# A four-layer graph network on one core: second pass in a new order, step values loaded by turns, top-8 rounds in pieces of 832 columns

## The reference, cut to what matters

```python
e = leaky_relu(e, 0.2)                                   # 4 heads, by edge
mask = topk_mask(e, row, 8)                              # 8 largest of each node and head
e = where(mask, e, -inf)
ez = exp(e - segment_max(e, row)[row])
alpha = ez / segment_sum(ez, row)[row]
out = elu(segment_sum(alpha[:, :, None] * x_j, row))
x = layernorm(x + out)
```

## Time and profile before

| | us |
|---|---|
| median of 3 timed runs | 14784.25 (14783.6 to 14784.43) |
| the profiled execution | 14750.02 |
| its span | 14748.2 |
| second pass, first turn to last scatter | 3636 to 10346 |
| top-8 rounds | 12660 to 13263 |
| last gather | 14561 |

### The profile page before, as it was taken

How to read it: one execution, slowest core, us unless ns; L and a number is a source line. 1 busy time by engine, 2 the same in 40 slices (tenths; PEclk the granted TensorE clock), 3 DMA queues, 4 the chain that set the end, 5 groups by cost and what they waited for, 6 DMA issues and landing times. The chain is left out here.

```text
span 14748.2 us, 216662 instructions
## 1 busy us (share of the span) xinstructions
PE 7244.2 (49%) x43137; PEld 6163.1 (42%) x43138; DVE 7073.5 (48%) x13194; ACT 1344.8 (9%) x4579; POOL 6702.6 (45%) x7772
## 2 busy tenths in 40 slices
PE   6999995673222222222222222223599578207543
PEld 4787774562222222222222222223366367206433
DVE  6444445776222222222222222222488678997535
ACT  1111111111000000000000000000011100001000
POOL 3777771663222222222222222225588057897773
PEclk9999998996555555555555555555799689657655
DMA  4777773451111111111111111114998069318654
GB/s 131 204 207 205 205 204 87 137 153 58 60 59 62 59 62 61 60 62 59 61 59 61 59 62 59 60 59 153 163 257 257 10 179 259 102 38 225 189 157 124
DMA packets 2114489, 1742.91 MB, mean 118 GB/s; under 512 B 377267, under 2 KB 1838644, under 8 KB 2114212
## 3 DMA queue, kind: packets, MB, share of 16 engines
q1 hardware_dynamic: 1220182, 819.70, 19.1%
q10 hardware_dynamic: 708032, 472.39, 12.2%
q0 software_dynamic: 186160, 449.72, 11.1%
HBM read 1289.54 MB, written 453.29 MB: 118 GB/s over the span
## 5 line engine op out<-in xcount | busy, mean ns | idle before, releaser
L1125 POOL DMA_INDIRECT sorted<-m_rows,srci x1612 | 1569.9, 974 | 5166.8 <-SPq L1112 4731.6
L1181 PE MATMUL m_psx<-held,m_hot 128*128 x3608 | 939.7, 441 | 4740.7 <-DVE m_rows L1335 4740.7
L1181 PEld LDWEIGHTS m_psx<-held,m_hot 128*128 128x128 f32 x3608 | 807.9, 329 | 4816.2 <-issue 4816.1
L1324 DVE TENSOR_SCALAR m_hot<-m_keys,node 128x512 f32<-128x512 int32 x451 | 225.7, 500 | 4583.0 <-DMA m_keys<-dst_row 4569.8
L1577 POOL DMA_INDIRECT z_xg<-table,srci x1664 | 2082.5, 1252 | 507.2 <-issue 507.2
L443 POOL DMA_INDIRECT g_xg<-table,srci x1612 | 1607.0, 997 | 491.1 <-issue 461.6
L1637 PE MATMUL z_ps<-z_wrow,z_oh 128*128 128x132 f32 x3712 | 757.8, 372 | 619.1 <-DVE z_wrow L1790 313.9
L462 PE MATMUL g_psg<-g_wg,g_eT 128*128 128x136 f32 x3224 | 1027.5, 474 | 0.0
L1452 PE MATMUL n_ps<-n_row,n_oh 128*128 128x257 f32 x3712 | 899.0, 391 | 249.4 <-DVE n_row L1428 203.4
L1637 PEld LDWEIGHTS z_ps<-z_wrow,z_oh 128*128 128x128 f32 x3712 | 666.7, 269 | 710.2 <-issue 670.2
L479 PE MATMUL g_psx<-scores,g_hot 128*128 x3608 | 840.2, 362 | 92.4 <-DVE e_score L568 87.0
(11 more groups left out here) (404 smaller groups left out, 13807.4 us busy)
## 6 DMA issues: line engine op xcount, KB each, us to landing
n_row<-sorted SPq DMA_DIRECT2D x464, 520.0 KB
z_buf<-gathered ACTq DMA_DIRECT2D x464, 256.0 KB, 3.6
g_keys<-dst_row ACTq DMA_DIRECT2D x451, 256.0 KB
ag_buf<-gated SPq DMA_DIRECT2D x451, 256.0 KB, 2.8
m_keys<-dst_row ACTq DMA_DIRECT2D x451, 256.0 KB, 3.7
gathered<-z_xg SPq DMA_DIRECT2D x416, 256.0 KB
gated<-g_y SPq DMA_DIRECT2D x403, 256.0 KB
g_eT<-in_attr_t SPq DMA_DIRECT2D x402, 256.0 KB
```

What stands on the lines that cost most here:

```text
L1125: nc.gpsimd.indirect_dma_start(out=v.sorted[:, :], out_offset=bass.IndirectOffsetOnAxis(ap=place[:, t:t + 1], axis=0), in_=rows[:, u, j, : ...
L1181: last = nc.tensor.matmul(psx[u % 2][:, j // 2, (j % 2) * WH:(j % 2 + 1) * WH], hot_t[:, u, j * P:(j + 1) * P], flat(held[:, ds(b, 1), :]) ...
```

## The change

It has four parts. (1) In the second pass the parts stand in a new order and with other lags. (2) `earlier` moves from DVE to ACT: PE first writes the triangle minus one into the bank by a matmul with the identity, the products are added on top, and ACT applies Relu. (3) `StepRow` loads the step values of a whole turn of the ring (4 or 8 steps, and those still needed from before) at its head, in place of one value at a time. In the second pass this is done on ACT and DVE, and in both aggregations on every engine that used `step_of`. (4) In the last layer, scans and knock-outs are cut into pieces of 832 columns of one head.

```diff
+class StepRow:
+    def turn(self, k, u):
+        if isinstance(k, int) or u:
+            return
+        _, self.values = self.nc.values_load_multi_w_load_instructions(
+            self.steps[0:1, self.row, ds(k - self.back, self.ring + self.back)], engines=[self.eng.engine], min_val=0,
+            max_val=self.top, skip_runtime_bounds_check_because=self.sure)
+    def at(self, k, u, lag=0):
+        if isinstance(k, int):
+            return self.eng.value_load(self.steps[0:1, self.row, ds(k, 1)], min_val=0, max_val=self.top)
+        return self.values[(u + lag) % self.ring - lag + self.back]
...
+                    nc.tensor.matmul(psq[:, :], ident[:, :], apart[:, None, :].broadcast_to([P, G, P]), start=True,
+                                     stop=False)
...
-                pipeline(pe, GE, (expand, 1, KE), (lookups, 3), (same, 1), (counts, 0), ring=R)
+                pipeline(pe, GE, (lookups, 3), (same, 1), (counts, 0), (expand, 1, KE), ring=R)
...
+                def earlier(g, u, use):
+                    if later(g, R):
+                        act.wait_ge(s_look, g - R + 1)
+                    act.wait_ge(s_q, g + 1)
+                    nc.scalar.activation(qm[:, u, :, :], tiles(psq[:, :]), ACT.Relu).then_inc(s_qm, 1)
...
-                pipeline(act, GE, (spread, 0, KE), (turned, 0), (high, 1), (middle, 2), (index, 5), (put, 6, KE), ring=R)
+                pipeline(act, GE, (spread, 0, KE), (turned, 2), (high, 2), (earlier, 2), (middle, 3), (index, 6), (put, 7, KE), ring=R)
...
-                def earlier(g, u, use):
-                    if later(g, R):
-                        dve.wait_ge(s_look, g - R + 1)
-                    dve.wait_ge(s_q, g + 1)
-                    nc.vector.tensor_tensor(qm[:, u, :, :], tiles(psq[:, :]),
-                                            v.before[:, None, :].broadcast_to([P, G, P]), ALU.mult).then_inc(s_qm, 1)
...
-                pipeline(dve, GE, (hot, 0, KE), (below_middle, 3), (choose, 4), (onehots, 0), (running, 1),
-                         (below_high, 2), (earlier, 2), (position, 4), (fill, 3, KE), ring=R)
+                pipeline(dve, GE, (hot, 0, KE), (fill, 3, KE), (below_middle, 3), (choose, 4), (onehots, 0), (running, 1),
+                         (below_high, 2), (position, 4), ring=R)
...
-        seg = Segments(nc, v, mem, "zs", fl, V)
+        seg = Segments(nc, v, mem, "zs", fl, V, pieces=2)
```

More of the change, by code:

```diff
@@ L346, in step_of, with __init__ @@
     return g, b
-class Blocks:
-    def __init__(self, nc, eng, steps, groups, lag, ring):
-        self.nc, self.eng, self.steps, self.groups, self.lag, self.ring = nc, eng, steps, groups, lag, ring
-        self.held = {}
-    def load(self, k, u):
-        g, b = step_of(self.nc, self.eng, self.steps, k, self.groups)
-        self.held[u] = b
-        return g, b
-    def again(self, k, u):
-        if isinstance(k, int) or u + self.lag >= self.ring:
-            return step_of(self.nc, self.eng, self.steps, k, self.groups)
-        b = self.held[u]
-        return self.nc.s_assert_within(k - b, 0, self.groups - 1,
-                                       skip_runtime_bounds_check_because="stage_steps makes group + block = step"), b
+class StepRow:
+    def __init__(self, nc, eng, steps, row, top, back, ring, waited=False):
+        self.nc, self.eng, self.steps, self.row, self.top = nc, eng, steps, row, top
+        self.back, self.ring = back, ring
+        self.sure = None if waited else "stage_steps keeps groups and blocks in their ranges"
+    def turn(self, k, u):
[8 more added lines that the diff above has]
+        return self.values[(u + lag) % self.ring - lag + self.back]
 def stage_gate(nc, v, e_score, gated, hist, steps):
@@ L673, with __init__ @@
 class Segments:
-    DVE, PE = 10, 4
-    def __init__(self, nc, v, mem, name, fl, V=None):
+    PE = 4
+    def __init__(self, nc, v, mem, name, fl, V=None, pieces=1):
         self.nc, self.v, self.fl, self.heads = nc, v, fl, fl.heads
         H = fl.heads
+        self.DVE = 2 * pieces + 8
+        self.cuts = [(n * TR // pieces, (n + 1) * TR // pieces) for n in range(pieces)]
         sb = lambda m, sh: mem.enter_context(nc.sbuf_tensor(name + m, sh, F32))
@@ L806, in _ @@
             def _(sp):
+                group = StepRow(nc, sp, steps, 0, groups - 1, 0, R)
                 def loads(k, u, use):
-                    g, _ = step_of(nc, sp, steps, k, groups)
+                    group.turn(k, u)
+                    g = group.at(k, u)
                     load(sp, k, u, g)
@@ L814, in _ @@
             def _(pool):
+                group = StepRow(nc, pool, steps, 0, groups - 1, 0, R)
                 def weighted(k, u, use):
-                    g, _ = step_of(nc, pool, steps, k, groups)
+                    group.turn(k, u)
+                    g = group.at(k, u)
                     if later(k, R):
@@ L825, in _ @@
                 nc.vector.memset(acc[:, :, 0:width], 0.0).then_inc(s_z, 1)
-                blocks = Blocks(nc, dve, steps, groups, 3, R)
+                group = StepRow(nc, dve, steps, 0, groups - 1, 0, R)
+                node = StepRow(nc, dve, steps, 1, NBX - 1, 3, R)
                 def prepare(k, u, use):
-                    g, b = blocks.load(k, u)
+                    group.turn(k, u)
+                    node.turn(k, u)
+                    g, b = group.at(k, u), node.at(k, u)
                     if later(k, R):
@@ L852, in _ @@
                 nc.scalar.preload_act_table(ACT.Copy)
+                group = StepRow(nc, act, steps, 0, groups - 1, 0, R)
                 def put(k, u, use):
-                    g, _ = step_of(nc, act, steps, k, groups)
+                    group.turn(k, u)
+                    g = group.at(k, u)
                     if later(k, R):
@@ L1222, in put @@
                 def put(k, u, use):
-                    g = act.value_load(steps[0:1, 0, ds(k, 1)], min_val=0, max_val=GE - 1)
-                    slot = act.value_load(steps[0:1, 2, ds(k, 1)], min_val=0, max_val=S - 1)
+                    g, slot = ahead.at(k, u, 7), slots.at(k, u, 7)
                     act.wait_ge(s_free, g + 1)
@@ L1317, in position @@
                                             ALU.add).then_inc(s_pos, 1)
+                node = StepRow(nc, dve, steps, 1, NBX - 1, 0, R)
+                group, slots = StepRow(nc, dve, steps, 0, GE - 1, 3, R, waited=True), StepRow(nc, dve, steps, 2, S - 1, 3, R)
                 def hot(k, u, use):
-                    b = dve.value_load(steps[0:1, 1, ds(k, 1)], min_val=0, max_val=NBX - 1)
+                    for row in (node, group, slots):
+                        row.turn(k, u)
+                    b = node.at(k, u)
                     if later(k, U):
```

94 lines of the change are left out of this document (60 added, 34 removed).

## The result

The changed kernel takes **10674.08 us** (median of 4 runs, 10659.52 to 10704.01) beside 14784.34 of the kernel before (14783.6 to 14791.5, 4 runs): a ratio of 0.7222, 95% interval 0.7204 to 0.7240. The profiled execution has a span of 10657.6 us against 14748.2, 4090.6 less.

What follows compares the result with a forecast made beforehand. Four parties waiting in a circle bound the second pass, 16.0 us a turn. Savings of 4352 (second pass), 50 (first aggregation) and 175 (last layer) from 14750.02 give 10173, plus 24: 10200 us; own case 9800 to 10500, range up to 11000.

Steps and rivals of the forecast that it cites:

- The new order breaks the circle: Second pass: keys requested before waiting for PE's work of that turn; turn from 16.0 to 5.2 us, 4352 us saved.
- The rival of a circle still closed in one turn: Second pass: some part still waits for its own turn's keys; 9.7 us a turn, 12010 us in all, chance 0.08.
- "I take 1.6" for ACT's block: Second pass: ACT's bundled loads at the head of four turns cost 1.6 us, 0.4 a turn; bounds 1.0 and 6.6.
- my 4.85 us for the rest of the turn: Second pass: turn length without ACT's bundled loads, from a two-turn chain of 9.4 to 10.0 us, 4.7 to 5.0 each.
- bundles cost by the value: Rival: each bundled value costs a full load; ACT block 6.6 us, turn 6.5, 10975 us in all, chance 0.12.
- First aggregation: Bundled loads replace single ones in steps of eight; 0.9 us by 56 turns, 50 us saved, or 200 lost if per value.
- The mask: Second pass: moving `earlier` (0.60 us) off DVE costs ACT as much and shortens a DVE turn that no longer bounds.
- Top-8 rounds: Last layer: pieces cost 35 us of starts but let 40 gathers through a round instead of 21; 175 us saved.
- DVE's wait for keys: Second pass, sign of being right: DVE waits under 1.5 us a turn for key numbers.
- A value-load block of over 3 us: Second pass, sign of being wrong: ACT's bundled value loads take over 3 us.
- gathers that end with every second border: Top-8 rounds, sign of being wrong: POOL's gathers still end with every second or later border between DVE instructions.
- POOL held by a denser DVE: Rival, second pass: each scatter waits some 0.35 us more; 5.8 us a turn, 10440 us in all, chance 0.10.

Runs made afterwards that it cites:

- lean kernel: Changed kernel with second-pass step values mostly loaded from multiples of four and no asserts on ACT: 10193.06 us; 10135.66 with DVE's block row aligned in both aggregations too.
- experiment 9: Lean kernel with ACT's second-pass parts put back to the lags of the kernel before: 14683.94 us, ratio 0.8572, on the slower kind of chip.
- experiment 5: Changed kernel with second-pass ACT loads of 4, 8 and 8 values from multiples of four, no asserts on ACT, and DVE's loads cheapened: 10193.06 us, ratio 0.6911.
- experiment 7: Kernel before the change, old order kept, with only the second pass's value loads bundled by `StepRow`: 14583.93 us, ratio 0.9885.
- experiment 3: Changed kernel with second-pass step values loaded one at a time again, new order kept: 13661.52 us, ratio 0.7978, on the slower kind of chip.
- experiment 6: Kernel of experiment 5 with DVE's block row in both aggregations also beginning at a multiple of four: 10135.66 us, ratio 0.6873.
- experiment 10: Lean kernel with the mask `earlier` back on DVE and no added matmul: 13443.0 us, ratio 0.7849, on the slower kind of chip.
- experiment 4: Changed kernel with the top-8 rounds whole again, without pieces: 10836.71 us (ratio 0.7353) on the faster kind of chip, 13771.3 (0.8040) on the slower.

## Why the prediction was right, and where it was off

The time came out inside the range, 4.6% above the number. By its steps, against the 4091 us of the two profiled executions (4577 foreseen):

- **The new order breaks the circle: right, and shown.** Keys are asked for ahead of anything TensorE makes in that turn, and the old lags alone bring back a turn of 10.2 us where the lean kernel has 6.7 (experiment 9). The rival of a circle still closed in one turn is out. The prediction takes the order as one term. By experiment 9 the lags are worth 1440 us, and more than that seems to come from the place of the parts on PE and DVE. The cheap bundles then give 5.06 us (experiment 5), where the prediction had 4.7 to 5.0 and 0.4 for bundles.
- **"I take 1.6" for ACT's block: the step that failed.** It measured 8.4 us. It even passed the upper bound of 6.6, because the assert was priced by its 0.018 alone. The kernel before had a second row at L1223, a register instruction of 0.15 us (x588 for 451 asserts), that I did not take in; by the block's rows an assert with its gap costs 0.23. And I counted 22 asserts where the code has 11. The loads of 11 values cost 2.9 each, close to my bound of a full load per value. The turn is 6.31, not 5.2: 447 of the 486 us that are missing.
- **Some luck in the size.** With my 4.85 us for the rest of the turn, a block of 8.4 in four turns would have given 6.95, 260 us more than was measured. It did not, because the turns without a block took 4.1, 4.9 and 4.1 us: that term was too large by some 0.5, which hid a part of the error in the block.
- **The rival "bundles cost by the value" was the true one for this term**, with 10975 us and a chance of 0.12. The result lies 301 below it: the turn is 6.31 and not 6.5 (77 us), and its loss in the first aggregation did not come. Of the two bundles there the one of 8 begins at a multiple of four and takes 0.59 us, only the one of 11 takes 2.5. The Trainium skill, "Runtime: NRT & Kernel Launch", section "Instruction fetch mechanics", gives some 200 ns a register even in bulk, from HBM. The loads from SBUF here agree with it, at 0.21 us, wherever they begin off a multiple of four, and not where they begin on one (12 values in 0.79).
- **Value loads: a gain in the old order, a loss in the new one.** Bundles saved 165 us in the old order (experiment 7, first chip); in the new order the change's bundles cost 169 us beside single loads (experiment 3, second chip). The likely reason, not tested apart, is that a block holds up keys for four turns at once, where the single loads lay beside other waits.
- **First aggregation: 50 us foreseen, 30 measured, and even that is not safe.** The same code took 742 us in the changed kernel and 773 in the lean one of experiment 5 (2642.9 to 3415.9), which is the time of before. The granted clock was 0.87 in the one and 0.76 in the other; whether that makes the difference was not tested. With 12 values from a multiple of four (experiment 6) it took 724, at 0.99.
- **The mask: right in direction, and of more use than I said.** I wrote that on DVE it shortens a turn that no longer bounds. On the second chip it does bound, by 0.55 a turn (experiment 10).
- **Top-8 rounds: right.** 35 us dearer foreseen, 34 measured; 40 gathers a round foreseen, 43 seen in one; 801 left foreseen, and 801 from the end of the last round at 9371.1; 175 us foreseen, 162 measured, and 163 by experiment 4. Of the two statements weighed from the Trainium skill, "SBUF — State Buffer", section "Who interferes with whom", the one on two SBUF inputs fits these gathers and the one on `tensor_tensor` does not.
- **The tail** was left as it is: 271 us.
- **Markers.** The clock (0.82), the DMA share (0.51), tail, gathers and rounds came as named. DVE's wait for keys was to be under 1.5 us a turn and is 870 / 403 = 2.2. "A value-load block of over 3 us" was named as a sign of being wrong, and it is the one that showed. Another sign, gathers that end with every second border, could tell nothing: the forecast of 40 a round assumes just that at borders 0.94 apart, and that is what came.
- **POOL held by a denser DVE**: no. Its scatters have a median of 0.96 us, the same as before.

## What to carry to other kernels

When every party of a loop waits for the next, find the request that starts the chain and issue it before anything its own turn must produce, and let no part stand behind a wait that it does not need. The new order as a whole made nearly all of the gain; by experiment 9 its lags alone were worth 1440 of 3890 us. Work that is taken out of each turn and put in one block at the head of four must be priced in full, with every row of its line, since it stands in front of the request. Load step values in groups of four from places that are multiples of four, load only those that are used, and assert only where a wait needs it: that took the time from 0.7222 to 0.6873 of that of the kernel before.

## What was unexpected in the hardware

- A register load from SBUF costs 0.32 us for 4 values and 0.79 for 12 from a multiple of four, 0.90 and 2.59 from one place further.
- The same kernel took 10837 us on one chip and 13771 on another. Whether that is the chip or what else ran on it, no run shows. The gate stage moved 205 GB/s on the one and 160 on the other, the scores stage 256 and 115. The top-8 rounds took 669 and 666 us.
- Neighbouring VectorE starts cost about 0.10 us each in the rounds when no gather runs (512 more starts, 53 us).
